# Another order for the first batch's preparation and the whole last batch, five weights' low parts on VectorE, and a wait on its own weights for each product

## The chip, the cores and the metric

The kernel runs on one core of a Trainium2 chip. The metric is the device time of one execution in microseconds (us). Five engines work in parallel, each through its own queue of instructions in order: TensorE (PE: matmuls and transposes; PEld is its weight load), VectorE (DVE), ScalarE (ACT), GpSimd (POOL) and SyncE (SP, which here issues the DMAs). They wait for one another by semaphores.

## The reference

x has 8 batches of 1024 tokens of 512 values. All tensors are float32.

```python
# attention-like part, on xn = layernorm(x)
s    = sigmoid(silu(xn @ s_w1.T + s_b1) @ s_w2.T + s_b2)        # 512 -> 256 -> 128
u    = (xn @ B_w.T + B_b) * s                                   # 128 states
h[t] = h[t-1] @ A.T + u[t]                                      # scan over the 1024 tokens
y    = h @ C_w.T + C_b + xn @ D_w.T + D_b
gate = sigmoid(xn @ g_w.T + g_b)
x1   = x + layernorm(y * gate)
# feed-forward part, on x2 = layernorm(x1)
z    = square(relu(x2 @ Ws1)) @ Ws2  + routed part
out  = x1 + layernorm(z)
```

The routed part is multiplied by the whole part of a softmax weight, so it is not zero only where one expert takes a weight of 1. A bound on the gap between router columns (`router_gap`, `route_flag`) says whether that can be, and with the given weights the branch that computes it is not entered.

## The kernel before

**Tiles.** A batch is 8 tiles of 128 tokens (index j, 0 to 7), in two halves of 4 tiles (index m). Each product of float32 values is made of three passes at the single-pass type: high part times high part, high times low, low times high (`mm3`, L428 to L430). So every weight needs a high part (ScalarE, `high_part`, L797) and a low part (raw minus high, `low_part`, L182), and every activation that goes into a product too.

**Work of one batch.** By the names in the code:
- `ln1_stats`, `ln1_norm` (VectorE, L1083 to L1099), with `ln1_rs` (GpSimd, L1533, a power) between them: the first layer norm, for the four tiles of a half at once in `ln1_rs`.
- `FT(j)` (TensorE, four transposes, L488), `ft_hi(j)` (ScalarE, L843), `ft_low(j)` (VectorE, L1161): the transposed tile in two parts.
- `H(m,f)` (12 matmuls over a half), `sig(m,f)` (ScalarE, L861), `h1(m,f)` (VectorE, L1177 and L1183), `h1_low(m,f)` (GpSimd, L1578), `B(m)` (12 matmuls), `SG(m)` (6 matmuls, L576 to L579), `s_gate(m)` (ScalarE, L869), `u_of(m)` (VectorE, L1192).
- The scan: 12 steps, each of a few small matmuls (`scan_step`) and one addition on VectorE (`scan_add`), strictly one after the other. Steps 5 to 11 give u[0] to u[6], and `hs(j)` (ScalarE), `hs_low(j)` (VectorE, L1137) split them for `Y`.
- `G(j)` (12 matmuls) and `gate(j)` (ScalarE, L812); `Y(j)` (15 matmuls: 12 of D, then 3 of C, which need `hs_low(j)`); `attn(j)` (VectorE, L1144, product and statistics), `v_rs(j)` (GpSimd), `attn_norm(j)` (VectorE, L1152), `x1(j)` (GpSimd, L1569, the residual), `x1_stats(j)` (VectorE), `x1_rs(j)` (GpSimd), `x1_norm(j)` (ScalarE, L835), `T(j)` (TensorE, four transposes), `t_hi(j)` (ScalarE, L830), `t_low(j)` (VectorE).
- `W1f(m,f)` (12 matmuls), `hidden(m,f)` (ScalarE, relu L852 and square L855), `h2(m,f)` (VectorE, L1207 and L1211), `W2(j)` (6 matmuls), `z_stats(j)` (VectorE), `z_rs(j)` (GpSimd), `zn(j)` (ScalarE, L874), `outs(j)` (GpSimd, L1573), store.

**Stages.** Before the first batch stands its preparation (layer norm, transposes, H, B, SG), together with 24 powers of A (`power(i)`, L438 on TensorE, `copy_power(i)`, L801 on ScalarE; each power needs the copy of the one before) and the parts of the weights. Then come `first_tail` and `body` for batch 0, `tail` and `body` for batches 1 to 6, and `last_tail`, `last_body` and a few last lines for batch 7. A `tail` holds the scan, G(0) to G(3) and the second half of the feed-forward part of the batch before; a `body` holds Y, G(4) to G(7), T, the first half of the feed-forward part and the preparation of the next batch. `last_tail` and `last_body` have no next batch to prepare. In each of these functions the order is written out by hand, for each engine.

**Buffers that set waits.** G, Y and z share three PSUM banks in a fixed ring (`TM_RING`, L209), T and FT two, H, B, SG and W1f two. `hs_hi` and `hs_lo` have two places. Raw weights lie in buffers that batches use later: s1, b, c, f1 and f2 in `work`, g and d in `xres`, s2 in `u`; so `gate(j)` of batch 0 waits for low parts that read `work[:, j]`, and the loads of `xres` (one_pass, L362) for those of g and d.

**Weights.** `less_first_of(name)` (VectorE, L1109) takes the first row off s1, b, g and d, and writes a bias into row 0 for g and d. The low parts of b and s2 are made on VectorE, those of s1, g, d, c, f1 and f2 on GpSimd. TensorE waits for the parts of s1, b, s2 before H, B, SG, for those of g before `first_tail`, and for all others, up to f2, before `body` of batch 0. VectorE too waits for the low part of f2 there.

**Order of the preparation before**, where pN is power(N), cN its copy, and hi and lo are parts of a weight:

```
PE   p0-5 FT0 p6 FT1 p7 FT2 p8 FT3 p9 p10 H00 p11 H01 p12 FT4 p13 B0 p14 FT5 p15 SG0 p16 FT6 p17 FT7 p18 p19
     H10 p20 H11 p21 B1 p22 SG1 p23 first_tail
ACT  c0-4 hi(s1) c5 ft_hi0 c6 ft_hi1 c7 ft_hi2 c8 ft_hi3 c9 c10 hi(b) hi(s2) hi(g) sig00 c11 sig01 c12 ft_hi4
     c13 c14 ft_hi5 c15 [wait less_first d] s_gate0 c16 ft_hi6 c17 ft_hi7 hi(d) c18 c19 sig10 c20 hi(c) hi(f1)
     sig11 c21 hi(f2) c22 s_gate1 c23 first_tail
DVE  stats0-3 norm0-3 less_first(s1) ft_low0 ft_low1 stats4 ft_low2 ft_low3 stats5 stats6 less_first(b) stats7
     lo(b) lo(s2) less_first(g) h1_00 norm4 h1_01 norm5-7 ft_low4 less_first(d) ft_low5 u_of0 ft_low6 ft_low7
     h1_10 h1_11 u_of1 first_tail
POOL rs0 lo(s1) rs1 h1_low00 h1_low01 lo(g) h1_low10 h1_low11 lo(d) lo(c) lo(f1) lo(f2)
```

## Time and profile before

| | |
|---|---|
| median of 3 runs | 909.72 us (908.83 to 910.61) |
| profiled execution | 909.91 us, span from first to last instruction 908.1 us |
| mean granted TensorE clock | 0.98 |
| busy in the span | PE 855.5, PEld 707.2, DVE 604.4, ACT 301.2, POOL 384.1 us |
| DMA | 73.23 MB, mean 81 GB/s |

The execution's own time is 1.8 us more than its span. Matmuls are pipelined, so a busy PE is not PE at its peak. The mean clock hides stages: a stretch of the trace runs at either 1.2 or 2.4 GHz, which the rows below show as a share of full speed (0.50 or 1.00, or a mixture where it changed inside).

### The profile page before, as it was taken

The page shows a single profiled execution, that of the slowest core. Times are in us where ns is not written, and L with a number is a line of the kernel's source. Part 1 is how long each engine was busy: PE and PEld are TensorE (multiplying, and loading weights), DVE is VectorE, ACT ScalarE, POOL GpSimd, SP SyncE. Part 2 cuts the span into 40 slices and gives each one's busy share as a digit, 9 for nine tenths or more (in the row PEclk, how much of TensorE's full clock was granted, in tenths as well). Part 3 has the DMA queues.
Part 4 walks back from the last instruction along what each step waited for, and adds up shares of the span by engine and source line. Part 5 has one row for each costly group of instructions (what it writes and reads, how often), then busy time and mean ns, then how long its engine had stood idle before and what let it go on. Part 6 is the DMA issues. An engine that isn't in the chain of part 4 may idle for free. (4 is left out here: it accounts for less than half of the span.)

```text
span 908.1 us, 12877 instructions
## 1 busy us (share of the span) xinstructions
PE 855.5 (94%) x4120; PEld 707.2 (78%) x4120; DVE 604.4 (67%) x1376; ACT 301.2 (33%) x530; POOL 384.1 (42%) x505
## 2 busy tenths in 40 slices
PE   5688999999999999999999999999999999999974
PEld 3566888888888888888888888888888888887763
DVE  4825677577766677577775777577785777744663
ACT  3241243323342233323343233332433233423332
POOL 1433344353461643444451633625443534605444
PEclk9879999999999999999999999999999999999987
DMA  9212022221132232302322220402222110122112
GB/s 296 75 49 92 1 93 93 93 70 52 65 117 71 93 92 80 107 24 70 93 93 94 93 90 19 150 22 93 93 93 94 61 75 4 70 70 93 48 46 93
DMA packets 17309, 73.23 MB, mean 81 GB/s; under 512 B 2643, under 2 KB 5075, under 8 KB 11094
## 3 DMA queue, kind: packets, MB, share of 16 engines
q1 hardware_dynamic: 17238, 72.38, 23.0%
q8 instruction: 33, 0.54, 0.3%
q14 instruction: 38, 0.31, 0.1%
HBM read 38.82 MB, written 33.55 MB: 80 GB/s over the span
## 5 line engine op out<-in xcount | busy, mean ns | idle before, releaser
L1533 POOL TENSOR_TENSOR rsz<-rsz,negh 128x1 f32<-128x1 f32 x64 | 39.9, 623 | 157.7 <-DVE rsz L1234 157.7
L428 PE MATMUL TM<-gw_hi,xT_hi 128*128 128x512 f32 x256 | 104.7, 409 | 0.7 <-ACT apt L801 0.7
L1569 POOL TENSOR_TENSOR xres<-work,xres 128x512 f32<-128x512 f32 x64 | 82.5, 1289 | 50.4 <-DVE work L1152 49.6
L428 PE MATMUL TM<-dw_hi,xT_hi 128*128 128x512 f32 x256 | 103.5, 404 | 0.0
L430 PE MATMUL TM<-dw_hi,xT_lo 128*128 128x512 f32 x256 | 100.6, 393 | 0.0
L430 PE MATMUL TM<-gw_hi,xT_lo 128*128 128x512 f32 x256 | 100.5, 393 | 0.0
L429 PE MATMUL TM<-dw_lo,xT_hi 128*128 128x512 f32 x256 | 100.1, 391 | 0.0
L429 PE MATMUL TM<-gw_lo,xT_hi 128*128 128x512 f32 x256 | 99.9, 390 | 0.0
L1533 POOL TENSOR_TENSOR rsv<-rsv,negh 128x1 f32<-128x1 f32 x64 | 35.9, 560 | 141.1 <-DVE rsv L1148 141.1
L1573 POOL TENSOR_TENSOR work<-work,xres 128x512 f32<-128x512 f32 x62 | 80.3, 1306 | 15.7 <-ACT work L874 15.7
L812 ACT ACTIVATE work<-TM 128x512 f32<-128x512 f32 x64 | 38.0, 594 | 121.3 <-PE TM L430 100.8
L874 ACT ACTIVATE work<-TM,nmz,rsz 128x512 f32<-128x512 f32 x62 | 48.3, 779 | 75.8 <-POOL nmz L1543 75.7
L1144 DVE TENSOR_TENSOR work<-TM,work 128x512 f32<-128x512 f32 x64 | 44.1, 689 | 39.9 <-PE TM L430 34.8
L830 ACT ACTIVATE x2T_hi<-TR 128x512 fp32r<-128x512 f32 x64 | 37.9, 594 | 77.6 <-PE TR L488 77.3
L1533 POOL TENSOR_TENSOR rsx<-rsx,negh 128x1 f32<-128x1 f32 x64 | 40.2, 628 | 54.0 <-DVE rsx L1158 54.0
L428 PE MATMUL TM<-f2w_hi,h_hi 128*128 128x512 f32 x124 | 51.8, 418 | 8.8 <-DVE h_lo L1211 6.9
L835 ACT ACTIVATE work<-xres,nmx,rsx 128x512 f32<-128x512 f32 x64 | 52.0, 812 | 24.2 <-POOL nmx L1543 24.2
L1578 POOL TENSOR_TENSOR h_lo<-hf,h_hi 128x512 fp32r<-128x512 f32 x32 | 41.7, 1303 | 38.5 <-DVE h_hi L1183 38.5
L430 PEld LDWEIGHTS TM<-dw_hi,xT_lo 128*128 128x128 f32 x256 | 48.3, 189 | 10.5
L430 PEld LDWEIGHTS TM<-gw_hi,xT_lo 128*128 128x128 f32 x256 | 48.0, 188 | 10.8
L428 PEld LDWEIGHTS TM<-gw_hi,xT_hi 128*128 128x128 f32 x256 | 48.2, 188 | 9.4 <-ACT apt L801 0.9
L429 PEld LDWEIGHTS TM<-dw_lo,xT_hi 128*128 128x128 f32 x256 | 48.5, 189 | 9.0
(145 smaller groups left out, 2104.4 us busy)
## 6 DMA issues: line engine op xcount, KB each, us to landing
...
```

Source lines behind the costliest of these rows:

```text
L428: eng.matmul(ps, lhs[0], rhs[0], start=first, stop=False)
L429: eng.matmul(ps, lhs[0], rhs[1], start=False, stop=False)
L430: return eng.matmul(ps, lhs[1], rhs[0], start=False, stop=last)
L812: eng.activation(work[:, j, :], tm_bank(f"g{j}")[:, :], ACT.Sigmoid).then_inc(S["gate_ok"], 1)
L830: eng.activation(x2T_hi[:, j % MS, :, :], tr_bank(f"t{j}")[:, :].rearrange("p (k n) -> p k n", n=P), ACT.Copy).then_inc(S["t_hi"], 1)
L835: eng.activation(work[:, j, :], xres[:, j, :], ACT.Identity, bias=nmx[:, j:j + 1], scale=rsx[:, j:j + 1])\
L874: eng.activation(work[:, j, :], z_bank(rep, j)[:, :], ACT.Identity, bias=nmz[:, j:j + 1], scale=rsz[:, j:j + 1]).then_inc(S["zn_ok"], 1)
L1144: eng.tensor_tensor(work[:, j, :], tm_bank(f"y{j}")[:, :], work[:, j, :], ALU.mult)\
L1533: return eng.tensor_tensor(dst, src, negh[:, 0:n], ALU.pow)
L1569: eng.tensor_tensor(xres[:, j, :], work[:, j, :], xres[:, j, :], ALU.add).then_inc(S["x1_ok"], 1)
L1573: eng.tensor_tensor(work[:, j, :], work[:, j, :], xres[:, j, :], ALU.add).then_inc(S["out_ok"], 1)
L1578: eng.tensor_tensor(h1_lo[:, f, :], hf_row(name), h1_hi[:, f, :].bitcast(F32), ALU.subtract).then_inc(S["h1lo_ok"], 1)
```

## The change

It does these things:
- The low parts of s1, g and d go from GpSimd to VectorE, so five are made there (s1, b, s2, g, d) and three on GpSimd (c, f1, f2).
- TensorE waits for the parts of each weight at the first product that reads them (`weights(name)`), and no longer for g before `first_tail` and for f2 before `body`. VectorE's wait for f2 goes. The wait for the copies of all powers stands at scan step 0. ScalarE's wait for less_first(d) before s_gate0 goes (it waits for that of g); VectorE adds the C and D biases by one operation of its own, `add_biases`, and d's row 0 is then a copy.
- The preparation, `first_tail`, `last_tail`, `last_body` and what follows them have another order on all four engines. `router_gap` moves on VectorE from before `last_tail` into it, and on TensorE from before the last four W2 to before the last one. `route_flag` stands before z_stats(7).
- The last z4 and z5 use other PSUM banks (TM[0] and TM[1] in place of TM[2] and TM[0]).

`tail` and `body`, which run batches 0 to 6, keep their order.

```
preparation after
PE   p0-5 FT0 p6 FT1 p7 FT2 p8 p9 FT3 p10-15 H00 FT4 p16 H01 B0 FT5 FT6 SG0 p17 FT7 p18 p19
     H10 p20 H11 p21 B1 p22 SG1 p23 first_tail
ACT  c0-5 hi(s1) ft_hi0 c6 c7 ft_hi1 c8-10 ft_hi2 c11-13 ft_hi3 c14 hi(b) c15 ft_hi4 hi(s2) sig00 hi(g) sig01
     c16 ft_hi5 ft_hi6 s_gate0 c17 ft_hi7 c18-20 sig10 c21 sig11 hi(d) hi(c) c22 hi(f1) c23 hi(f2) s_gate1
DVE  stats0-3 less_first(s1) norm0 norm1 lo(s1) norm2 ft_low0 norm3 stats4 stats5 ft_low1 stats6 ft_low2 ft_low3
     stats7 add_biases less_first(b) norm4 less_first(g) lo(b) h1_00 norm5 h1_01 norm6 lo(s2) ft_low4 ft_low5
     norm7 ft_low6 u_of0 ft_low7 lo(g) less_first(d) h1_10 h1_11 lo(d) u_of1 first_tail
POOL rs0 rs1 h1_low00 h1_low01 h1_low10 h1_low11 lo(c) lo(f1) lo(f2)
last_tail | last_body | what follows (norm is attn_norm)
PE   G0{s0} s1 W10{s2} W11{s3 s4} s5 G1{s6} s7 G2{s8} W2_4 s9 W2_5 s10 G3 W2_6 W2_7 s11 |
     Y0 G4 Y1 G5 Y2 G6 Y3 T0 G7 Y4 T1 Y5 T2 T3 Y6 W00 Y7 W01 T4 T5 W2_0 W2_1 T6 T7 W2_2 W2_3 |
     W10 W11 W2_4 W2_5 W2_6 router_gap W2_7
ACT  (body) hs2 hs3 gate4 x1_norm0 gate5 t_hi0 hs4 hs5 gate6 x1_norm1 x1_norm2 hs6 gate7 t_hi1 x1_norm3 hs7 t_hi2
     t_hi3 x1_norm4 hidden00 x1_norm5 t_hi4 hidden01 t_hi5 x1_norm6 x1_norm7 t_hi6 zn0 t_hi7 zn1 zn2 |
     hidden10 hidden11 zn3 zn4-7
DVE  (body) attn0 hs_low2 norm0 x1_stats0 attn1 hs_low3 attn2 norm1 norm2 x1_stats1 attn3 t_low0 norm3 x1_stats2
     hs_low4 x1_stats3 attn4 hs_low5 hs_low6 t_low1 norm4 attn5 t_low2 t_low3 norm5 hs_low7 x1_stats4 x1_stats5
     attn6 h2_00 norm6 attn7 x1_stats6 norm7 t_low4 h2_01 x1_stats7 t_low5 z_stats0 z_stats1 t_low6 t_low7
     z_stats2 z_stats3 | h2_10 h2_11 z_stats4-6 route_flag z_stats7 last residuals (j = 6, 7)
POOL (body) in pairs: v_rs0 x1_0 x1_rs0 v_rs1 x1_1 v_rs2 x1_2 x1_rs1 v_rs3 x1_3 x1_rs2 x1_rs3 v_rs4 x1_4 v_rs5 x1_5
     x1_rs4 x1_rs5 v_rs6 x1_6 v_rs7 x1_7 x1_rs6 x1_rs7 z_rs0 outs0 z_rs1 z_rs2 outs1 outs2 z_rs3 |
     outs3 z_rs4 z_rs5 outs4 outs5 z_rs6 z_rs7
```

The diff, cut to its core (of the orders only some stand here; the lists above hold the rest). The low parts, the banks and TensorE's waits and `first_tail`:

```diff
-        LO_DVE = {n: i + 1 for i, n in enumerate(["b", "s2"])}
-        LO_POOL = {n: i + 1 for i, n in enumerate(["constants", "s1", "g", "d", "c", "f1", "f2"])}
+        LO_DVE = {n: i + 1 for i, n in enumerate(["s1", "b", "s2", "g", "d"])}
+        LO_POOL = {n: i + 1 for i, n in enumerate(["constants", "c", "f1", "f2"])}
-        LAST_BANKS = dict(zip(range(MS, L), (TM[2], TM[0], *TR)))
+        LAST_BANKS = dict(zip(range(MS, L), (TM[0], TM[1], *TR)))
...
+            def weights(name):
+                eng.wait_ge(hi_ok, HI[name])
+                eng.wait_ge(*lo_of(name))
             def scan_step(b, rep, i):
+                if i == 0 and rep == 0:
+                    eng.wait_ge(pw_cp, len(POWERS))
...
             def G(b, rep, j, steps={}):
+                if rep == 0 and j == 0:
+                    weights("g")
             def Y(b, rep, j):
+                if rep == 0 and j == 0:
+                    weights("d")
+                    weights("c")
...
             def first_tail(b, rep):
-                G(*a, 0, {2: 0, 3: 1})
-                G(*a, 1, {0: 2, 1: 3, 2: 4, 3: 5})
-                G(*a, 2, {0: 6, 1: 7, 2: 8, 3: 9})
-                G(*a, 3, {0: 10, 1: 11})
+                G(*a, 0, {1: 0})
+                scan_step(*a, 1)
+                G(*a, 1, {0: 2, 1: 3, 2: 4})
+                scan_step(*a, 5)
+                G(*a, 2, {1: 6, 2: 7})
+                scan_step(*a, 8)
+                scan_step(*a, 9)
+                G(*a, 3, {0: 10})
+                scan_step(*a, 11)
...
-            eng.wait_ge(pw_cp, len(POWERS))
-            eng.wait_ge(hi_ok, HI["g"])
-            eng.wait_ge(lo_pool, LO_POOL["g"])
             first_tail(0, 0)
-            eng.wait_ge(hi_ok, HI["f2"])
-            eng.wait_ge(lo_pool, LO_POOL["f2"])
             body(0, 0)
```

VectorE's `first_tail` (up to step 8), `last_tail` (from step 6) and the end of `last_body`:

```diff
             def first_tail(b, rep):
                 scan_add(*a, 0)
                 ln1_stats(b + 1, 0)
                 scan_add(*a, 1)
+                ln1_stats(b + 1, 1)
                 scan_add(*a, 2)
-                ln1_stats(b + 1, 1)
+                ln1_stats(b + 1, 2)
                 scan_add(*a, 3)
                 scan_add(*a, 4)
+                ln1_stats(b + 1, 3)
                 scan_add(*a, 5)
                 scan_add(*a, 6)
-                ln1_stats(b + 1, 2)
+                ln1_norm(b + 1, 0)
                 scan_add(*a, 7)
-                ln1_stats(b + 1, 3)
                 scan_add(*a, 8)
...
             def last_tail(b, rep):
...
                 scan_add(*a, 6)
+                hs_low(*a, 0)
+                h2(*a, 1, 1)
                 scan_add(*a, 7)
+                router_gap()
                 scan_add(*a, 8)
-                hs_low(*a, 0)
                 scan_add(*a, 9)
                 z_stats(*a, 4)
+                z_stats(*a, 5)
                 scan_add(*a, 10)
-                hs_low(*a, 1)
-                z_stats(*a, 5)
-                scan_add(*a, 11)
                 z_stats(*a, 6)
                 z_stats(*a, 7)
+                hs_low(*a, 1)
+                scan_add(*a, 11)
             def last_body(b, rep):
...
                 attn(*a, 6)
+                h2(*a, 0, 0)
                 attn_norm(*a, 6)
-                h2(*a, 0, 0)
+                attn(*a, 7)
                 x1_stats(*a, 6)
-                attn(*a, 7)
                 attn_norm(*a, 7)
+                t_low(*a, 4)
                 h2(*a, 0, 1)
-                t_low(*a, 4)
                 x1_stats(*a, 7)
```

ScalarE, after `last_body`:

```diff
             hidden(NB, NB, 1, 0)
+            hidden(NB, NB, 1, 1)
             zn(NB - 1, NB - 1, 3)
-            hidden(NB, NB, 1, 1)
```

## Rows read from the trace of the kernel before

**Rows 1.** Busy us and (x) instructions by engine, PE's clock: first and last stretch.

```profile
110.00:210.00 100.00, 99.86 (x490) 82.91 (x489) 70.66 (x165) 33.39 (x59) 44.45 (x61) 1.00 0.24 85
...
710.00:790.00 80.00, 79.66 (x385) 66.05 (x383) 60.63 (x137) 28.34 (x50) 41.35 (x58) 1.00 0.14 53
```

**Rows 2.** Who waited for whom, PE: us in total, times, longest.

```profile
PE SC L438 <- ACT apt L801: 12.1, 7, 4.5
```

**Rows 3.** In order of time, PE, preparation: start, duration, what, [idle before].

```profile
7.95 0.79 PE L438 MATMUL SC<-apt,u 128*128 128x128 f32 x2 [0.37 <-ACT u L801]
9.11 0.79 PE L438 MATMUL SC<-apt,u 128*128 128x128 f32 x2 [0.37 <-ACT apt L801]
...
22.09 0.47 PE L428 MATMUL FM<-xT_hi,s1w_hi 128*128 128x512 f32 x1 [0.16 <-DVE xT_lo L1161]
...
51.47 0.77 PE L428 MATMUL FM<-xT_hi,s1w_hi 128*128 128x512 f32 x1
...
52.47 0.63 PE L430 MATMUL FM<-xT_hi,s1w_lo 128*128 128x512 f32 x1
52.90 0.63 PE L428 MATMUL FM<-xT_hi,s1w_hi 128*128 128x512 f32 x1
...
66.92 1.72 PE L448 MATMUL SC<-u,apt 128*128 128x128 f32 x14
...
86.42 1.08 PE L488 MATMUL TR<-ident,xin 128*128 128x128 f32 x4 [3.78 <-DVE xin L1099]
```

**Rows 4.** In order of time, ACT: copy_power(4), high_part(s1), s_gate(0).

```profile
12.26 0.28 ACT L801 ACTIVATE apt<-SC 128x128 f32<-128x128 f32 x1 [0.89 <-PE SC L438]
15.10 1.06 ACT L797 ACTIVATE s1w_hi<-work 128x1024 fp32r<-128x1024 f32 x1 [2.56 <-DVE work L1109]
...
45.82 0.69 ACT L869 ACTIVATE sg<-FM,b_col 128x512 f32<-128x512 f32 x1 [4.70 <-DVE xres L1116]
```

**Rows 5.** Groups, DVE, 0 to 66 us: shapes, count, busy, mean ns.

```profile
L1099 DVE TENSOR_SCALAR xin<-xin,mv,rs 128x511 f32<-128x511 f32 x8 | 9.1, 1192 | 1.2 <-issue 1.2
L1083 DVE BATCH_NORM_STATS2 st<-xin 128x6 f32<-128x512 f32 x8 | 5.5, 690 | 5.7 <-DMA xin<-in_x 5.1
L1109 DVE TENSOR_TENSOR xres<-xres,w_first 128x2048 f32<-128x2048 f32 x2 | 4.6, 2280 | 0.0
L1161 DVE TENSOR_TENSOR xT_lo<-TM,xT_hi 128x512 fp32r<-128x512 f32 x6 | 4.1, 686 | 4.2 <-ACT xT_hi L843 4.1
L1177 DVE SCALAR_TENSOR_TENSOR hf<-FM,b_col,hf 128x512 f32<-128x512 f32 x4 | 3.0, 750 | 11.6 <-ACT hf L861 11.6
```

**Rows 6.** In order of time, DVE norms, then POOL h1_low and lo(g).

```profile
35.48 6.68 DVE L1099 TENSOR_SCALAR xin<-xin,mv,rs 128x511 f32<-128x511 f32 x3
...
35.64 1.51 POOL L1578 TENSOR_TENSOR h_lo<-hf,h_hi 128x512 fp32r<-128x512 f32 x1 [0.36 <-DVE h_hi L1183]
37.11 4.76 POOL L182 TENSOR_TENSOR gw_lo<-xres,gw_hi 128x2048 fp32r<-128x2048 f32 x1
```

**Rows 7.** In order of time, PE, the last batch.

```profile
817.99 0.50 PE L428 MATMUL TM<-f2w_hi,h_hi 128*128 128x512 f32 x1 [1.24 <-ACT work L874]
...
854.47 0.63 PE L488 MATMUL TR<-ident,work 128*128 128x128 f32 x4 [1.98 <-ACT work L835]
...
867.29 1.03 PE L488 MATMUL TR<-ident,work 128*128 128x128 f32 x8
872.98 0.79 PE L428 MATMUL TM<-f2w_hi,h_hi 128*128 128x512 f32 x1 [4.66 <-DVE h_lo L1211]
...
882.65 0.39 PE L428 MATMUL FM<-x2T_hi,f1w_hi 128*128 128x512 f32 x1
...
888.12 1.00 PE L527 MATMUL SC<-w_first 128*128 128x64 f32 x8
891.38 0.78 PE L428 MATMUL TM<-f2w_hi,h_hi 128*128 128x512 f32 x1 [2.26 <-DVE h_lo L1211]
```

**Rows 8.** In order of time, DVE: the last residual.

```profile
904.14 0.69 DVE L1487 TENSOR_TENSOR work<-work,xres 128x512 f32<-128x512 f32 x1 [1.72 <-ACT work L874]
```

More of the change, by code:

```diff
@@ L511, in W1f @@
                     eng.wait_ge(S["t_lo"], body_at("t_lo", i, m * MS + MS - 1))
+                if rep == 0 and f == 0:
+                    weights("f1")
                 wait_free(eng, FM_RING, name, b, rep, FM_FREED)
@@ L536, in W2 @@
                     eng.wait_ge(S["h2lo_ok"], body_at("h2lo_ok", i, KF * m + KF - 1))
+                if rep == 0 and j == 0:
+                    weights("f2")
                 if rep < NB or j < MS + 2:
@@ L549, in H @@
                 name = f"h{m}{f}"
+                if rep < 0 and (m, f) == (0, 0):
+                    weights("s1")
                 if f == 0:
@@ L562, in B @@
                 js = slice(m * MS, (m + 1) * MS)
+                if rep < 0 and m == 0:
+                    weights("b")
                 wait_free(eng, FM_RING, f"b{m}", b, rep, FM_FREED)
@@ L569, in SG @@
             def SG(b, rep, m):
+                if rep < 0 and m == 0:
+                    weights("s2")
                 wait_free(eng, FM_RING, f"s{m}", b, rep, FM_FREED)
@@ L753, in _ @@
             last_body(NB - 1, NB - 1)
-            for f in range(KF):
-                W1f(NB, NB, 1, f)
+            W1f(NB, NB, 1, 0)
+            W1f(NB, NB, 1, 1)
+            W2(NB, NB, 4)
+            W2(NB, NB, 5)
+            W2(NB, NB, 6)
             router_gap()
-            for j in range(MS, L):
-                W2(NB, NB, j)
+            W2(NB, NB, 7)
             def routed_ffn(w1, w2):
@@ L859, in sig @@
                 eng.wait_ge(S["h_done"], prep_at("h_done", b + 1, KF * m + f))
+                if rep < 0 and (m, f) == (0, 0):
+                    eng.wait_ge(w_ld["small"], 3 * 16)
+                elif rep < 0 and (m, f) == (0, 1):
+                    eng.wait_ge(less_first, LESS_FIRST["b"])
                 wait_free(eng, HF_RING, name, b, rep, HF_FREED)
@@ L865, in s_gate @@
                 eng.wait_ge(S["s_done"], prep_at("s_done", b + 1, m))
+                if rep < 0 and m == 0:
+                    eng.wait_ge(less_first, LESS_FIRST["g"])
                 if m or rep >= 0:
@@ L1050, in _ @@
             hidden(NB, NB, 1, 0)
+            hidden(NB, NB, 1, 1)
             zn(NB - 1, NB - 1, 3)
-            hidden(NB, NB, 1, 1)
-            for j in range(MS, L):
-                zn(NB, NB, j)
+            zn(NB, NB, 4)
+            zn(NB, NB, 5)
+            zn(NB, NB, 6)
+            zn(NB, NB, 7)
             def routed_ffn():
@@ L1228, in route_flag, with last_outs @@
                    .then_inc(flag_ok, 1)
+            def last_outs(i):
+                j = L - 2 + i
+                eng.wait_ge(S["zn_ok"], body_at("zn_ok", NB - 1, j))
+                eng.tensor_tensor(work[:, j, :], work[:, j, :], xres[:, j, :], ALU.add).then_inc(last_out, 1)
             def z_stats(b, rep, j):
@@ L1476, in _ @@
                 body(b, 1)
-            router_gap()
             last_tail(NB - 1, NB - 1)
@@ L1481, in _ @@
             h2(NB, NB, 1, 1)
-            for j in range(MS, L):
-                z_stats(NB, NB, j)
-            for j in (L - 2, L - 1):
-                eng.wait_ge(S["zn_ok"], body_at("zn_ok", NB - 1, j))
-                eng.tensor_tensor(work[:, j, :], work[:, j, :], xres[:, j, :], ALU.add).then_inc(last_out, 1)
+            z_stats(NB, NB, 4)
+            z_stats(NB, NB, 5)
+            z_stats(NB, NB, 6)
             route_flag()
+            z_stats(NB, NB, 7)
+            last_outs(0)
+            last_outs(1)
             def routed_norm(dst, src):
```

317 lines of the change are left out of this document (167 added, 150 removed).

## Prediction, made before the changed kernel ran

> **What bounds the kernel now.** I read the busy time by stretch first. From 110 to 790 us, six middle batches, PE is busy for 99.86 of the first 100 us and 79.66 of the last 80, at a granted clock of 1.00, seven stretches alike [rows 1]. No order on another engine can shorten that part, and the change leaves it alone. So what can be won lies in the first 90 us and after 790. There I read PE's waits: 12.1 us for ScalarE's copies of powers, 7 times, 4.5 at most [rows 2], and then the instructions in order of time. In the preparation H(0,0) starts at 22.09, H(1,0) at 51.47, scan step 0 at 66.92, and FT(0) of the next batch, at 86.42, had waited 3.78 us for VectorE [rows 3]. H(1,0) is so late because of ScalarE's queue: s_gate(0) started at 45.82 after a wait of 4.70 for less_first(d) on VectorE [rows 4], and less_first(d) stood behind three norms that took 6.68 us together [rows 6]. In the last batch PE waits 1.24, 1.98, 4.66 and 2.26 us [rows 7]. Each stall of over 2 us costs twice: behind one, matmuls started 0.43 us apart (52.47 to 52.90) [rows 3], where 24 of them at full clock take 5.47 us (882.65 to 888.12), 0.23 each [rows 7].
>
> **The preparation up to H(0,0): a loss.** Before, powers 11 to 15 lay between products; now they stand ahead of H(0,0), and nothing covers them. One power and its copy are a round trip of 1.16 us (7.95 to 9.11) [rows 3]. Copy 4 starts at 12.26 [rows 4], copy 5 at 13.4; then hi(s1), 1.06 [rows 4], and one transposed high part of about 0.6 (estimate: a little under the 0.69 of s_gate) put copy 6 at 15.1. Nine more round trips, 10.4 us, bring power 15 to 25.5. ft_hi3 now stands behind copy 13, so ft_low3 ends at about 25.6, and H(0,0) starts at 26.2: 4.1 us later than before. lo(s1) is not late for it: half the columns of the VectorE pass that takes 2.28 us [rows 5], 1.2 us, from 14.7. The bounds of a round trip: its two durations alone, 0.79 and 0.28, give 1.07 (0.8 us less); if every one also waits for a high part of 0.6, 5.4 us more. I take 1.16, the row of the same pair of instructions.
>
> **From H(0,0) to H(1,0): the gain.** 24 matmuls, 5.5 us, with eight of them at the slow clock (8 x 0.2 = 1.6, since PE has had little to do before) and FT(4) with power 16 (0.8) end H(0,1) at 34.1. Then sig (0.7), h1 (0.75 and a cast of 0.4) [rows 5] and h1_low(0,1) with 1.51 [rows 6] run while PE does B(0), FT(5), FT(6). SG(0) starts at 39.0, since lo(s2) stands on VectorE behind norm6 and meets that h1_low. SG(0) 1.4, s_gate 0.7, u_of 0.75, ft_hi7 0.6, ft_low7 0.69 [rows 4, 5]: H(1,0) at 43.2, against 51.47, so 8.3 us earlier. What goes is the wait of s_gate(0) for less_first(d), and GpSimd's lo(g) of 4.76 us with the norms that stood still in it [rows 6]. lo(g) and lo(d) on VectorE have no row before; the nearest are less_first(g) and (d), the same columns and engine, 2.28 us each [rows 5], and GpSimd's 4.76 [rows 6] is the upper bound. I take 2.28.
>
> At this place a rule of the Trainium skill can be weighed. The row: three norms took 6.68 us while h1_low and lo(g) ran on GpSimd, and the other five of the eight, 9.1 - 6.68, took 0.48 each [rows 5, 6]. The Trainium skill (SBUF — State Buffer, section "SBUF: two separate sides") says that VectorE's two-port operations, and those with two SBUF inputs, share a port pair with GpSimd that one of them holds for its whole instruction. By that rule, the low parts now on VectorE stop GpSimd in turn, and lo(s2) waits for an h1_low as I put it; without the rule SG(0) and the sum would be 1.4 us earlier.
>
> **From H(1,0) to scan step 0.** 42 matmuls at 0.23 are 9.6 us, powers and starts add 1.2: power 23 ends at 54.0. Now ScalarE decides: s_gate(1) stands behind copy 23 and hi(f2). 0.3 + 1.06 + 0.7 + 0.75 [rows 4, 5] put u and step 0 at 56.8, against 66.92. Gain so far 10.1. On VectorE lo(g) runs at 43.1 to 45.4, less_first(d) with its row copy to 48.2, lo(d) ends at about 55.0; each is done before its product (G(0) at 54, Y(0) at 73), so they cost nothing while PE stays this late. If it were 9 us earlier, lo(g) would be the next to wait for. The new waits for single weights are met in the same way: c, f1, f2 on GpSimd (a quarter and twice a half of 4.76) end by 61.
>
> **first_tail and the next batch's FT(0).** Same 48 matmuls, same 12 steps; before they took 66.92 to 82.64 (86.42 less 3.78) [rows 3]. Steps 8 and 9 now stand together with nothing between: 0.3 us more. In return norm(0) of batch 1 stands behind scan_add 6 instead of 11 and behind statistics that fit between the steps (0.69 each and a small one) [rows 5], so FT(0) doesn't wait: 3.8 us, and the slow clock behind that wait, about seven matmuls and the transposes, 1.4 us. Start in all: 10.1 - 0.3 + 3.8 + 1.4 = **15.0 us**. The loads of xres can start earlier and nobody waits for them.
>
> **The last batch.** In last_tail W2(7) waited 1.24 us for zn(5) [rows 7]: z_stats(5) now stands ahead of scan_add 10 and hs_low(1): **1.2 us**. router_gap there takes about 2 us of VectorE between steps 7 and 8, while PE has three quarters of G(2): nothing. In last_body T(0) and T(1) come later, and x1_norm(3) stands ahead of hs(7), with GpSimd's work in pairs; by the same durations x1_norm(3) ends at about 851, before T(3) at 852.4, so 1.98 us go. Then h2(0,1) stands before x1_stats(7), and W2(0) waits about 2.7 us instead of 4.66: gain 4.0. Between W2(0) and W1f(1,0) another 0.64 of a wait for zn(0), by my placing of it, and three slow matmuls go: 1.2, so 5.2. hidden(1,1) no longer stands behind zn(3), and the router's product (1.00) [rows 7] leaves the gap between 888.12 and 891.38: 1.0 earlier, of which 0.5 comes back before W2(7). On GpSimd outs(5) stands before z_rs(6), 1.3 us that the others mostly hide: 0.3. The last residual, at 904.14 [rows 8], moves by 5.2 + 1.0 - 0.5 + 0.5 (a slow stretch a little shorter) - 0.3 = about **6 us**. The 0.64 and these halves are estimates from the same rows; a stall that isn't shortened takes them away, one that vanishes gives up to 2.7 more.
>
> **Sum.** 15.0 + 1.2 + 6.2 = 22.4 us. Against the profiled execution's 909.91 us that is 887.5. It stands 0.2 above the median of the runs shown (909.72), so I forecast 887.3.
>
> **Rivals.**
> - *The start gives half.* The round trips before H(0,0) take more than 1.16, or u(1) comes later behind hi(d), hi(c), hi(f1), hi(f2) and lo(d). For it: both chains are bare now, with 12.1 us of PE waits on copies already [rows 2]. Step 0 at 62 rather than 56.8, and a norm or two waiting for GpSimd: 5 to 9 us less gain, 893 to 897.
> - *The end gives nothing.* The last batch is a chain over five engines; if v_rs(2), now behind x1(1) on GpSimd, makes each hs_low late, PE waits at Y(4) to Y(7) for what it saved at T(3) and W2(0). 887.3 + 6 = 893.
> - *It doesn't do what it says.* PE bound in the middle could hold only if batch 1 needs something that comes at the old time, such as a load. The loads of x for batch 1 hang on FT(3) and FT(7) of batch 0, which come earlier. 909.7.
> - *Slower.* One mechanism in last_body: hs(4) stands on ScalarE behind t_hi(0), and that behind T(0), which PE now reaches only after Y(3); hs_low(4) on VectorE stands behind attn(3), norm3 and x1_stats(2), each behind a GpSimd step. If each of the five Y from Y(3) on waits for its hs_low, the change loses from 4.7 us apiece on (5 x 4.7 = 23.5, over the 22.4), which is the longest stall of the last batch before (4.66) [rows 7]: 911 and more. Against it: by my placing hs_low(4) is ready 0.7 us before Y(4) needs it.
>
> **How the numbers follow.** Forecast 0.61 (its own range 881 to 893: -1 to +3 at the round trips, 0 to 1.8 for the slow clock at each of three places, up to 2.7 at W2(0)); start gives half 0.20; end gives nothing 0.12; no effect 0.03; slower 0.04. The range reaches from 880 to 898 and leaves out some of the second rival with the last two. Faster 0.93, within 0.2% (about what a measurement of this kernel can tell) 0.03, slower 0.04.
>
> **What would show it.** In the profile after: H(0,0) near 26 and at the slow clock first; H(1,0) near 43; step 0 near 57; no wait for xin at FT(0); the middle still at 99% with 1.00; no wait of 1.98 at T(3); a wait under 3 us before W2(0); the last residual about 22 us earlier than 904. A step 0 later than 62, or waits for hs_low in the last Y, would make the forecast wrong.

## The result and the profile after

The changed kernel took **878.57 us** (median of 4 runs, 878.09 to 881.48) against 910.16 for the kernel before in the same session (4 runs), a ratio of 0.9662 with a 95% interval of 0.9638 to 0.9686. It is faster, as forecast, and by more than forecast: 31.6 us where 22.4 were summed, and below the range of 880 to 898. The profiled execution took 878.09 us, its span 876.3.

The page's line of busy time, and then who waited for whom on PE (us in total, times, longest):

```profile
PE 846.2 (97%) x4120; PEld 699.9 (80%) x4120; DVE 600.0 (68%) x1380; ACT 299.5 (34%) x530; POOL 374.5 (43%) x502
```

```profile
PE TM L433 <- DVE h_lo L1257: 4.4, 2, 2.3
...
PE SC L443 <- ACT apt L828: 2.4, 7, 0.4
...
PE SC L459 <- DVE u L1238: 1.4, 1, 1.4
PE TM L433 <- DVE hs_lo L1181: 1.1, 6, 0.2
```

The waits for copies of powers into `apt`, 12.1 us with one of 4.5 before [rows 2], are 2.4 now, seven of at most 0.4 (with the copies into `u` and `carry`: 15.1 before, 4.6 now). The waits for norms went from 4.6 to 0.3, the one of 2.0 at T(3) for x1_norm(3) is gone, and the two for h2's low part went from 6.9 to 4.4 us. The middle is nearly what it was: from 100 to 770 us PE is busy for 666.34 of 670 us (665.39 before), at a granted clock of 1.00; its one wait per batch for hs_low is 0.18 us in place of 0.34.

In order of time, PE in the preparation:

```profile
7.75 0.79 PE L443 MATMUL SC<-apt,u 128*128 128x128 f32 x2 [0.37 <-ACT u L828]
8.91 0.79 PE L443 MATMUL SC<-apt,u 128*128 128x128 f32 x2 [0.37 <-ACT apt L828]
...
19.36 0.49 PE L443 MATMUL SC<-apt,u 128*128 128x128 f32 x2 [0.37 <-ACT carry L828]
20.22 0.49 PE L443 MATMUL SC<-apt,u 128*128 128x128 f32 x2 [0.37 <-ACT apt L828]
...
23.23 0.56 PE L433 MATMUL FM<-xT_hi,s1w_hi 128*128 128x512 f32 x1
23.59 0.63 PE L434 MATMUL FM<-xT_lo,s1w_hi 128*128 128x512 f32 x1
24.02 0.63 PE L435 MATMUL FM<-xT_hi,s1w_lo 128*128 128x512 f32 x1
...
35.36 0.47 PE L602 MATMUL FM<-h_hi,s2w_hi 128*128 128x512 f32 x1 [0.52 <-issue]
...
39.15 0.50 PE L433 MATMUL FM<-xT_hi,s1w_hi 128*128 128x512 f32 x1
...
52.76 1.80 PE L459 MATMUL SC<-u,apt 128*128 128x128 f32 x14 [1.37 <-DVE u L1238]
68.89 0.60 PE L504 MATMUL TR<-ident,xin 128*128 128x128 f32 x4
69.29 0.47 PE L433 MATMUL TM<-dw_hi,xT_hi 128*128 128x512 f32 x1
```

And in the last batch, with VectorE's last residual behind it:

```profile
843.96 1.03 PE L504 MATMUL TR<-ident,work 128*128 128x128 f32 x8
847.29 0.50 PE L433 MATMUL TM<-f2w_hi,h_hi 128*128 128x512 f32 x1 [2.30 <-DVE h_lo L1257]
847.63 0.40 PE L434 MATMUL TM<-f2w_lo,h_hi 128*128 128x512 f32 x1
...
853.83 0.39 PE L433 MATMUL FM<-x2T_hi,f1w_hi 128*128 128x512 f32 x1
...
861.57 0.50 PE L433 MATMUL TM<-f2w_hi,h_hi 128*128 128x512 f32 x1 [2.15 <-DVE h_lo L1257]
861.91 0.39 PE L434 MATMUL TM<-f2w_lo,h_hi 128*128 128x512 f32 x1
```

```profile
872.33 0.69 DVE L1279 TENSOR_TENSOR work<-work,xres 128x512 f32<-128x512 f32 x1 [0.29 <-ACT work L908]
```

Set against rows 3, 7 and 8, in us of the span (the gain in the last column is before less after):

| | before | forecast | after | gain |
|---|---|---|---|---|
| H(0,0) | 22.09 | 26.2 | 23.23 | -1.1 |
| H(1,0) | 51.47 | 43.2 | 39.15 | 12.3 |
| scan step 0 | 66.92 | 56.8 | 52.76 | 14.2 |
| FT(0) of batch 1 | 86.42 | | 68.89 | 17.5 |
| scan step 0 of the last batch | 792.51 | | 772.85 | 19.7 |
| transposes ahead of W2(0) | 867.29 | | 843.96 | 23.3 |
| W2(0) | 872.98 | | 847.29 | 25.7 |
| W1f(1,0) | 882.65 | | 853.83 | 28.8 |
| W2(4) | 891.38 | | 861.57 | 29.8 |
| last residual | 904.14 | | 872.33 | 31.8 |

So the start gave 19.7 us where 15.0 were summed, and the end 12.1 where 7.4 were. Two things in the rows stand out. The power round trip is 1.16 us early (7.75 to 8.91), as in the row that I used, but 0.86 later (19.36 to 20.22): the two matmuls take 0.49 in place of 0.79, the wait for the copy 0.37 both times. And behind the last two waits the matmuls follow at 0.23 us (granted clock 1.00), where before seven and then six of them stood 0.43 apart (granted clock 0.50). Such a run of matmuls 0.43 us apart is called a slow stretch below.

### The profile page after: what moved, and what is told of

The parts are those of the page before. It is cut to its first block and busy times, and to the rows that moved or that the text cites. A ratio compares the mean times of both kernels' runs of the same rounds, so it can differ in the third digit from the quotient of the medians.

```text
span 876.3 us, 12884 instructions
## 1 busy us (share of the span) xinstructions
PE 846.2 (97%) x4120; PEld 699.9 (80%) x4120; DVE 600.0 (68%) x1380; ACT 299.5 (34%) x530; POOL 374.5 (43%) x502
## 5 line engine op out<-in xcount | busy, mean ns | idle before, releaser
L1628 POOL TENSOR_TENSOR work<-work,xres 128x512 f32<-128x512 f32 x62 | 79.5, 1293 | 17.5 <-ACT work L908 17.5
L1188 DVE TENSOR_TENSOR work<-TM,work 128x512 f32<-128x512 f32 x64 | 44.0, 688 | 30.6 <-PE TM L435 29.8
L434 PEld LDWEIGHTS TM<-gw_lo,xT_hi 128*128 128x128 f32 x256 | 48.3, 189 | 8.7
L433 PEld LDWEIGHTS TM<-dw_hi,xT_hi 128*128 128x128 f32 x256 | 48.1, 188 | 8.8
```

Source lines behind the costliest of these rows:

```text
L433: eng.matmul(ps, lhs[0], rhs[0], start=first, stop=False)
L434: eng.matmul(ps, lhs[0], rhs[1], start=False, stop=False)
L1188: eng.tensor_tensor(work[:, j, :], tm_bank(f"y{j}")[:, :], work[:, j, :], ALU.mult)\
L1628: eng.tensor_tensor(work[:, j, :], work[:, j, :], xres[:, j, :], ALU.add).then_inc(S["out_ok"], 1)
```

## Experiments

All are timed against the kernel before on the same chip (909.74 to 910.26 there), and "the changed kernel" is the 878.57 above, four executions that were not repeated beside the experiments. Ratios are to the kernel before, with 95% intervals; the changed kernel's is 0.9638 to 0.9686, so a difference from it of under about 2 us is not told apart from nothing by the medians alone. A comparison inside two profiles says more, but each is one execution.

### One end of the change at a time

**e1_last_only** is the kernel before with the new `last_tail`, `last_body`, what follows them, and the new banks. **e2_start_only** is the changed kernel with the old ones.

In e1 every engine has the new end behind the old preparation and `first_tail`; in e2 every engine has the old end behind the new preparation, `first_tail`, low parts and waits. The banks, in e1:

```diff
-        LAST_BANKS = dict(zip(range(MS, L), (TM[2], TM[0], *TR)))
+        LAST_BANKS = dict(zip(range(MS, L), (TM[0], TM[1], *TR)))
```

> The kernel before with only the new order of the last batch (last_tail, last_body and what follows, on all four engines, and the two banks). Theory: the changed kernel gained 19.7 us up to scan step 0 of the last batch (792.51 to 772.85) and 12.1 after it (31.8 at the last residual), and the two are independent, so this gives 910.2 - 12.1 = 898. Rival: my forecast's 7.4 is what the order gives, and the other 4.7 (slow-clock stretches behind the two last stalls that did not come) was luck of one execution or hangs on the start: 902.8, with matmuls 0.43 us apart behind a stall of over 2 us in the last batch.

> The changed kernel with the old order of the last batch, so only the preparation, first_tail, the low parts on VectorE and the waits for single weights are new. Theory of independent parts: 910.2 - 19.7 = 890.5. Rival (the start gives what I forecast, 15.0, and the middle batches gave the rest in one execution only): 895.

Measured: e1 899.49 us, ratio 0.9879 (0.9862 to 0.9895), a gain of 10.8. e2 889.15, ratio 0.9771 (0.9755 to 0.9787), 21.1. Together 31.9, against 31.6 for the whole change: the two ends add up, and each gave more than its part of the sum (7.4 and 15.0). "The end gives nothing" and "the start gives half" are both out. How the gain divides holds only within some 1.4 us, the size of a slow stretch: e1's profile has one behind W2(0), where the changed kernel's has none, and e2's has none behind W2(4), where the profile of before has one.

### Parts of the start

**e3_old_first_tail**: the changed kernel with the old order of `first_tail` on PE, ScalarE and VectorE.

VectorE, cut:

```diff
                 scan_add(*a, 6)
-                ln1_norm(b + 1, 0)
+                ln1_stats(b + 1, 2)
                 scan_add(*a, 7)
...
                 scan_add(*a, 11)
                 ln1_stats(b + 1, 5)
                 ln1_stats(b + 1, 6)
                 ln1_stats(b + 1, 7)
+                ln1_norm(b + 1, 0)
+                ln1_norm(b + 1, 1)
+                ln1_norm(b + 1, 2)
```

> The changed kernel with the old first_tail on all engines. Theory: norm(0) of batch 1 again stands behind scan_add 11 on VectorE, so FT(0) waits 3.8 us and the clock falls behind that wait (1.4): 878.6 + 5.2 - 0.3 = 883.5. Rival: first_tail was late before because the scan started late and weights were late; then the old order costs nothing here: 878.6.

887.56 us, ratio 0.974 (0.9719 to 0.9761): 9.0 us slower than the changed kernel, where the theory had 4.9. PE's rows have the wait back, with its slow clock:

```profile
73.63 1.08 PE L504 MATMUL TR<-ident,xin 128*128 128x128 f32 x4 [3.78 <-DVE xin L1134]
74.36 0.78 PE L433 MATMUL TM<-dw_hi,xT_hi 128*128 128x512 f32 x1
74.94 0.63 PE L434 MATMUL TM<-dw_lo,xT_hi 128*128 128x512 f32 x1
...
79.20 0.58 PE L435 MATMUL TM<-dw_hi,xT_lo 128*128 128x512 f32 x1
79.62 0.39 PE L433 MATMUL TM<-cw_hi,hs_hi 128*128 128x512 f32 x1
```

From 74.94 to 79.62 eleven matmuls stand 0.43 apart (granted clock 0.50), 0.2 us too many each: 2.2 us. That number is this execution's. Behind the same wait the kernel before had five:

```profile
88.58 0.63 PE L428 MATMUL TM<-dw_hi,xT_hi 128*128 128x512 f32 x1
89.01 0.53 PE L429 MATMUL TM<-dw_lo,xT_hi 128*128 128x512 f32 x1
89.38 0.39 PE L430 MATMUL TM<-dw_hi,xT_lo 128*128 128x512 f32 x1
```

From FT(0) to the first C product of Y(0) it is 5.99 us in e3, 4.56 in the kernel before and 3.25 in the changed kernel. From scan step 0 to that of the last batch e3 takes 726.14 us in place of 720.09, so the order of `first_tail` costs 6.0 us here. The profiled execution (888.47) is 10.4 us over the changed kernel's (878.09); the rest of that is slow stretches behind both last waits, 3.0 (next part but one), and 1.3 up to H(0,0), of which 1.1 is the load that power(0) waits for (7.73 in place of 6.59), not the edit.

**e4_early_waits** brings the early waits back: g ahead of `first_tail`, d and f2 ahead of `body` on PE, f2 on VectorE.

```diff
+            weights("g")
             first_tail(0, 0)
+            weights("d")
+            weights("f2")
             body(0, 0)
```

> The changed kernel with TensorE's old waits back: for g before first_tail, for d and f2 before body, and VectorE's for f2 before body. Theory: all of them are over by then (lo(f2) ends at 56.8, FT(0) starts at 68.9, lo(g) ends at 41.3, G(0) starts at 49.75), so 878.6. Rival (waiting for each product's own weights is a part of the gain): over 880.5.

878.82 us, ratio 0.9667 (0.9647 to 0.9686). No cost: each low part is done before either wait. The part "each product waits for its own weights" brings nothing in this order.

**e6_lows_on_pool** gives GpSimd the low parts of s1, g and d again.

```diff
-        LO_DVE = ... ["s1", "b", "s2", "g", "d"]
-        LO_POOL = ... ["constants", "c", "f1", "f2"]
+        LO_DVE = ... ["b", "s2"]
+        LO_POOL = ... ["constants", "s1", "g", "d", "c", "f1", "f2"]
```

> The changed kernel (878.6) with the low parts of s1, g and d back on GpSimd and all else as changed. Theory (the engine of these three matters: lo(g) took 4.76 us on GpSimd before, and VectorE's norms stood still for 6.68 in it): SG(0) or H(1,0) some 3 us later, 881 to 884. Rival (the order of the powers and products did it all, and the engine of the low parts nothing): 878.6.

886.35 us, ratio 0.9751 (0.9736 to 0.9767): 7.8 us slower, more than the theory's 2.4 to 5.4. GpSimd, and VectorE beside it:

```profile
34.51 4.72 POOL L186 TENSOR_TENSOR gw_lo<-xres,gw_hi 128x2048 fp32r<-128x2048 f32 x1
```

```profile
35.95 3.57 DVE L1139 TENSOR_SCALAR xin<-xin,mv,rs 128x511 f32<-128x511 f32 x1
```

The norm takes 3.57 us in place of 0.54 and ends 0.3 behind lo(g) (39.23). FT(6) waits 2.88 for it, H(1,0) comes at 41.70 (2.5 later) with a slow stretch behind it, and step 0 at 56.82 (4.1 later). Scan step 0 of the last batch is at 779.13, 6.3 later, and the end has a slow stretch behind W2(0), 1.5. The 2.2 between the two steps are not the low parts: those are made by 63.4. They come from one wait for hs_low in each of the six middle batches, at 199.96 and then every 104.8 us, 0.5 us in place of 0.2, and that from VectorE's own queue, which stands idle longer at one place of a batch whose order is the same. e6, then the changed kernel:

```profile
196.68 0.18 DVE L1124 BATCH_NORM_AGGREGATE mvv<-st 128x2 f32<-128x6 f32 x1 [0.50 <-DVEq L1120]
```

```profile
192.25 0.18 DVE L1124 BATCH_NORM_AGGREGATE mvv<-st 128x2 f32<-128x6 f32 x1 [0.15 <-DVEq L1120]
```

It is 0.50 and 0.15 in each of the six. What makes it so, no run shows. So by these profiles the engine of the low parts is worth 4.1 us of the start's 19.7, all of it before step 0, and the rest of the change there some 15.6; the 7.8 of the medians also holds the middle batches and the slow stretch. The Trainium skill (SBUF — State Buffer, section "SBUF: two separate sides") has VectorE's two-port operations shut out for a whole GpSimd instruction; the trace agrees, and in the changed kernel in both directions. There lo(d) meets h1_low(1,1), which GpSimd ends at 48.88, and GpSimd's lo(c) then meets lo(d); in e10, where it doesn't, lo(c) takes 1.32:

```profile
48.12 2.92 DVE L186 TENSOR_TENSOR dw_lo<-xres,dw_hi 128x2048 fp32r<-128x2048 f32 x1 [0.60 <-ACT dw_hi L824]
```

```profile
48.84 3.33 POOL L186 TENSOR_TENSOR cw_lo<-work,cw_hi 128x512 fp32r<-128x512 f32 x1
```

### The clock at the start

**e5_fillers** puts one unused matmul (into a bank that is overwritten) behind each of powers 9 to 15, which keeps PE busy during the copies. For power 9:

```diff
             power(9)
+            filler()
```

> The changed kernel (878.6) with one more matmul of 128x128 behind each of powers 9 to 15, in PE's waits of 0.37 us for the copies; its result goes to a bank that is overwritten. Theory (H(0,0)'s first nine matmuls are slow only because PE had little to do before): H(0,0) at 23.2 as before but its first matmuls 0.23 apart instead of 0.43, 1.6 to 1.8 us won, most of it kept up to scan step 0 only if ScalarE's chain there also moves: 877.0 to 878. Rival (the extra matmuls lengthen the round trips of 0.855 by 0.1 to 0.3 each, 1 to 2 us over seven): H(0,0) at 24 to 25 and 878.6 or more.

Busy time, granted clock next to last but two, from 23 to 27 us, in e5 and then in the changed kernel:

```profile
23.00:27.00 4.00, 3.73 (x19) 2.67 (x17) 3.46 (x9) 0.88 (x3) 1.38 (x1) 1.00 1.08 381
```

```profile
23.00:27.00 4.00, 4.00 (x12) 3.05 (x12) 3.47 (x9) 0.80 (x2) 1.38 (x1) 0.57 0.90 325
```

The slow matmuls of H(0,0) are gone, as the theory said, yet the time is 879.9 us (877.72 to 881.23), ratio 0.9669 (0.9655 to 0.9683): nothing won. From H(0,0) to SG(0) it is 11.63 us in place of 12.13, so of my 1.6 us for eight slow matmuls 0.5 were to be had; the rest lay beside other engines' work: B(0) now waits 0.48 us for h1(0,0), which stands on VectorE behind less_first(g), 2.28 us from 26.91 on. H(0,0) itself is at 23.86, 0.63 later, and so SG(0) is at 35.49 (35.36 without the fillers). The fillers don't do that: from power 11 on a round trip takes 0.86 us as without them (the rival's 0.1 to 0.3 more didn't come), but power 9, which stands ahead of the first of them, starts at 18.14 in place of 17.65, since PE reached the upper level later here. And this profile has a slow stretch behind W2(0), 1.5 us, which has nothing to do with the edit.

**e9_sgate_first** puts s_gate(1) ahead of hi(f2); **e10_sgate_d_pool** also gives lo(d) to GpSimd.

```diff
-            high_part("f2")
             s_gate(-1, -1, 1)
+            high_part("f2")
```

> The changed kernel (878.6) with s_gate(1) ahead of the high part of f2 on ScalarE. Theory (step 0 waits 1.37 us for u(1), that for s_gate(1) at 51.15, that for the high part of f2, 1.05): s_gate(1) about 0.95 earlier, u(1) then bound by lo(d), which ends at 51.04 on VectorE, so step 0 0.8 earlier: 877.8. Rival (lo(c) and lo(d), 3.33 and 2.92 beside each other, hold u(1) back anyway): 878.6.

> As the last one, and the low part of d on GpSimd ahead of that of c. Theory (u(1) is then free at s_gate(1)'s end): step 0 at 51.4 to 51.8, 877.2 to 877.6. Rival (GpSimd, as with three low parts on it, where PE waited 3.2 us for hs_lo in place of 1.1, is the bound behind step 0: its low parts end some 3 us later): the gain is given back in the first body, 878.6 to 880.7.

e9 took 878.97 us (ratio 0.9672, 0.9656 to 0.9687), e10 878.83 (0.9662, 0.9649 to 0.9675), with the lowest execution at 877.22 and the profiled one. The wait at step 0 shrank from 1.37 to 0.47 and 0.43, and from H(0,0) to step 0 it is 28.5 and 28.4 us in place of 29.5, but the medians don't show that microsecond. e9's profile says what hid it there: H(0,0) at 24.49. Of e10's rival the profiles show 0.3 us: from step 0 to that of the last batch 720.42 in place of 720.09, and its waits for hs_low are 1.1 us as in the changed kernel (those of e6 were not the low parts' doing, as above). What hid e9's gain stands in the profile of e7 (below) too, whose edit is 840 us later:

```profile
19.91 0.49 PE L443 MATMUL SC<-apt,u 128*128 128x128 f32 x2 [0.37 <-ACT carry L828]
20.76 0.53 PE L443 MATMUL SC<-apt,u 128*128 128x128 f32 x2 [0.37 <-ACT apt L828]
21.66 0.79 PE L443 MATMUL SC<-carry,apt 128*128 128x128 f32 x2 [0.37 <-ACT apt L828]
22.82 0.79 PE L443 MATMUL SC<-apt,carry 128*128 128x128 f32 x2 [0.37 <-ACT u L828]
```

The clock fell at 21 rather than at 23 (granted clock from 21 to 24 us 0.51), and the round trips behind it cost 1.16 us instead of 0.86. The order is the same. In the ten profiles with this order and no fillers (changed kernel, e2 to e4, e7 to e12) H(0,0) is anywhere from 22.99 to 24.55, and two things differ from one execution to the next: where the clock changes, and when the load that power(0) waits for is there (6.53 to 7.06 us, and 7.73 in e3).

### The clock and the orders at the end

**e7_gap_back** has `router_gap` ahead of W2(4) again, on PE alone. **e8_zn3_back** has ScalarE's zn(3) ahead of hidden(1,1) again.

e7, PE, and then e8, ScalarE:

```diff
+            router_gap()
             W2(NB, NB, 4)
             W2(NB, NB, 5)
             W2(NB, NB, 6)
-            router_gap()
```

```diff
             hidden(NB, NB, 1, 0)
+            zn(NB - 1, NB - 1, 3)
             hidden(NB, NB, 1, 1)
-            zn(NB - 1, NB - 1, 3)
```

> The changed kernel (878.6) with the router's product back ahead of W2(4), on PE alone. Theory (my forecast, which credited 1.0 us to moving it, of which 0.5 came back): W2(4) starts later by 0.5 to 1.0, 879.1 to 879.6. Rival (the product of 1.0 us lies inside the wait of 2.15 for h_lo and costs nothing there; what won the microsecond is ScalarE's zn(3), now behind hidden(1,1)): W2(4) at its old place, W2(7) 0.45 earlier, 878.1 to 878.6.

> The changed kernel (878.6) with zn(3) back ahead of hidden(1,1) on ScalarE, nothing else. Theory (this order is what shortened PE's idle time before W2(4), 3.26 with the router's product in it to 2.15): the wait before W2(4) grows by 0.8 to 1.1, 879.4 to 879.7, and with it a slow stretch of 1.6 us is likelier. Rival (the product's place did it): 878.6.

e7: 879.75 us (877.89 to 882.03), ratio 0.9666 (0.9649 to 0.9683). W2(4) follows the last product of W1f(1,1) in the same time as in the changed kernel, since the product lies inside the wait, which is 1.31 us now:

```profile
862.52 1.00 PE L545 MATMUL SC<-w_first 128*128 128x64 f32 x8
864.82 0.50 PE L433 MATMUL TM<-f2w_hi,h_hi 128*128 128x512 f32 x1 [1.31 <-DVE h_lo L1257]
```

and from W2(4) to the last residual it is 10.73 us (10.76 in the changed kernel). So the product's place, to which I gave 1.0 less 0.5, is worth nothing either way. e8: 882.05 us (880.92 to 882.57), ratio 0.9696 (0.9682 to 0.9709), 3.5 slower in the medians and 2.8 in the profiles: the wait before W2(4) grows to 3.12, 1.0 more, and eight matmuls behind it are 0.43 apart, 1.6 us. From W1f(1,0) to W2(4) it is 8.72 us there, 8.73 in the kernel before and 7.74 in the changed kernel. zn(3) behind hidden(1,1) is what won the microsecond, and in this profile more with the clock.

**How often the slow stretch comes.** Orders and waits at the end are alike in many of these kernels, so their profiles are repeats:

| wait | profiles | with 5 to 8 matmuls at 0.43 us behind it |
|---|---|---|
| 2.30, before W2(0) | 10 | 5 (e1, e3, e5, e6, e7) |
| 2.14 or 2.15, before W2(4) | 8 | 2 (e3, e4) |
| 2.26 (before), 2.28 (e2), before W2(4) | 2 | 1 (before) |
| 3.12 (e8), 4.66 (before, e2) | 3 | 3 |

So behind a wait of 2.14 to 2.30 us it came in 8 of 20. In e4 it begins 1.3 us after the product started:

```profile
860.62 0.50 PE L433 MATMUL TM<-f2w_hi,h_hi 128*128 128x512 f32 x1 [2.15 <-DVE h_lo L1260]
860.95 0.39 PE L434 MATMUL TM<-f2w_lo,h_hi 128*128 128x512 f32 x1
...
861.88 0.48 PE L435 MATMUL TM<-f2w_hi,h_lo 128*128 128x512 f32 x1
862.16 0.63 PE L433 MATMUL TM<-f2w_hi,h_hi 128*128 128x512 f32 x1
```

The granted clock, next to last but two, says that this is the clock and not a wait:

```profile
860.60:862.10 1.50, 1.48 (x6) 1.24 (x7) 0.00 (x0) 0.00 (x0) 1.20 (x1) 0.98 0.00 0
862.20:865.50 3.30, 3.30 (x9) 2.60 (x8) 1.57 (x4) 0.62 (x1) 0.81 (x2) 0.51 0.39 159
```

**e11_busy_stalls** puts six unused matmuls into each of the two waits; **e12_sgate_busy** has s_gate(1) earlier as well.

```diff
                 T(*a, 5)
+                busy(6)
                 W2(*a, 0)
...
             W1f(NB, NB, 1, 1)
+            busy(6)
             W2(NB, NB, 4)
```

> The changed kernel (878.6) with six matmuls of 128x128 put into each of PE's two last waits, ahead of W2(0) and W2(4), into a bank nobody reads there. Theory (a slow stretch of up to 8 matmuls, 1.6 us, comes behind these waits in some executions and not in others, as the profiles of the kernels above show; PE kept busy has none): no stretch at 0.43 us apart behind either, and the executions between 877.5 and 880, the median 878.0 to 878.6 with less scatter than 878.1 to 881.5. Rival (the scatter of 3 us comes from elsewhere, such as the start): the same scatter as before, 878.6.

> s_gate(1) ahead of the high part of f2, and the matmuls in both waits. Theory (the two add): 877.2 to 877.8, the candidate to beat the changed kernel. Rival (neither is on the path): 878.6.

e11: 878.12 us, ratio 0.9658 (0.9645 to 0.9671), four of its five executions from 877.74 to 878.3 and one at 880.55. No slow stretch at the end of its profile. The interval lies within the changed kernel's, and the changed kernel's own profile had no slow stretch either, so a gain from the fillers isn't shown. e12: 877.32 (876.93 to 879.4), ratio 0.9653 (0.964 to 0.9666). It differs from e11 by s_gate(1) alone and was timed on the same chip: step 0 is at 51.85 in place of 52.79, the last residual at 871.26 in place of 872.27, and the medians are 0.8 apart, though the executions overlap.

**e13_before_busy** does it to the kernel before: 13 and 6 unused matmuls in its two last waits, all orders untouched.

```diff
+                busy(13)
                 W2(*a, 0)
...
             router_gap()
+            busy(6)
```

> The kernel before with matmuls of 128x128 in PE's two last waits (13 ahead of W2(0), where it waits 4.66 us, 6 ahead of W2(4)), orders and waits untouched. Theory (the slow clock behind these waits was on the path to the end, 7 matmuls at 0.2 us each in the profile of before): no matmuls 0.43 us apart behind them, 1.4 to 2.8 us won, 907 to 908.5. Rival (the chain over the other engines, not PE's pace, sets the end): 909.8.

909.29 us, ratio 0.9992 (0.9983 to 1.0001): 0.7 us, which isn't told apart from nothing, and half of the theory's least. PE's rows:

```profile
870.63 3.07 PE L442 MATMUL SC<-ident 128*128 128x128 f32 x26
...
873.85 0.50 PE L428 MATMUL TM<-f2w_hi,h_hi 128*128 128x512 f32 x1 [0.15 <-DVE h_lo L1217]
...
882.03 0.50 PE L428 MATMUL TM<-f2w_hi,h_hi 128*128 128x512 f32 x1 [2.50 <-ACT work L880]
...
892.88 0.50 PE L428 MATMUL TM<-f2w_hi,h_hi 128*128 128x512 f32 x1
```

The two waits tell different things. The stretch behind W2(0) is gone and nothing is won there: PE waits 2.50 us at W2(3) for zn(0), in place of 0.64, and the clock falls behind that, so that W1f(1,0) comes 10.14 us after W2(0) in place of 9.67. ScalarE's zn(0) starts 7.35 us after W2(0) here and 7.33 in the kernel before, at either clock; in the changed kernel it is 4.19. The kernel before and then the changed kernel:

```profile
880.31 0.78 ACT L874 ACTIVATE work<-TM,nmz,rsz 128x512 f32<-128x512 f32 x1 [2.62 <-POOL nmz L1543]
```

```profile
851.48 0.78 ACT L908 ACTIVATE work<-TM,nmz,rsz 128x512 f32<-128x512 f32 x1
```

So before the change the path there went over the other engines (x1_norm(7), which waited 3.4 us for GpSimd, t_hi(5), t_low(5), z_stats(0), z_rs(0), zn(0)), not over PE. Behind W2(4) it is otherwise: with the stretch gone, the last residual (904.08) comes 11.20 us after W2(4), in place of 12.76. That stretch was on the path, 1.56 us. Over the whole last batch, from step 0 to the last residual, the profile has 110.76 us in place of 111.63, 0.9 less.

**e14_sgate_busy_fill** is e12 with one unused matmul behind each of powers 10 to 15.

```diff
             power(10)
+            filler()
```

> s_gate(1) ahead of the high part of f2, matmuls in both last waits, and one behind each of powers 10 to 15. Theory (what scatter is left comes from the clock at the start, where a fall ahead of power 13 costs 0.3 us per round trip): the executions within 1.5 us of each other, the median 876.9 to 877.3. Rival (the scatter is in what PE waits for elsewhere): 876.9 to 879.4 as without them.

876.64 us, ratio 0.9637 (0.9624 to 0.9651): three executions from 876.51 to 876.64, two at 878.43 and 878.5. It is 1.9 us below the changed kernel in the medians; the two intervals still overlap a little (0.9638 to 0.9651). The scatter didn't go: in the profiled execution, at 878.5, PE's pace reached the upper level only at 22 us (17 in the changed kernel), with PE busy for all of 20 to 22, and H(0,0) came at 25.13. In this profile and in e5's no matmul of H(0,0) is slow, in the ten without fillers six or seven are at 0.43. So matmuls between the powers kept the clock up once it had risen, but it still rose late here.

## Why the prediction was outside its range

The direction, both mechanisms and most of the places were right; terms of the sum were wrong, nearly all to one side. The start was 4.7 us too small (19.7 for 15.0) and the end 4.7 (12.1 for 7.4). Two steps failed: the price of a power round trip ahead of H(0,0), and "each stall of over 2 us costs twice", which kept slow stretches in the sum behind both last waits, and the first of them as PE's path.

- **The preparation up to H(0,0): a size wrong, 3.0 us.** "I take 1.16, the row of the same pair of instructions." It is the same pair, but a row at 8 us, and by 17 us PE ran at the upper of its two levels: seven of the nine round trips took 0.86, and from copy 6 (15.1 forecast, 15.09 measured) to the end of power 15 (23.27) it is 8.2 us, not 10.4. That is 2.2 of the 3.0. The other 0.7 is a gap that the sum left between power 15 (25.5) and H(0,0) (26.2) without a row for it; there is none. The evidence on the pace was in the trace of before: power 10 took 0.49 there, at 21.44. My lower bound of 1.07 was "its two durations alone", at the slow durations, so it was no bound: 0.86 is under it.
- **From H(0,0) to step 0: right within 1.1 us** (30.6 summed, 29.5 measured). The slow matmuls came as forecast and H(0,1) took as long as summed, 7.9 us from H(0,0); the 1.1 too many stand behind it, 0.6 up to SG(0) and 0.4 from there to H(1,0). "lo(s2) ... meets that h1_low" was right: it takes 1.49 us at 33.77, where it took 0.42 alone before. But it ends at 35.26, 0.3 behind h1_low(0,1) (34.97), which SG(0) at 35.36 needs too: by these rows it costs about 0.3, not the 1.4 put on it. "u and step 0 at 56.8" because of s_gate(1) behind hi(f2) was the right link: the wait is there, 1.37 us, and goes with the order (e9).
- **Low parts of s1, g and d on VectorE: right**, at 2.28 us for g; d takes 2.92, of which 0.64 beside h1_low(1,1). Their engine is worth 4.1 us up to step 0 (e6).
- **FT(0) of batch 1: right**, 3.4 by the rows for 3.8 less 0.3. **The slow clock behind it: right**, 1.3 for 1.4 (4.56 us from FT(0) to the first C product before, 3.25 after); e3 drew a longer one. **The batches after it: 0.8 where I had nothing.** "The change leaves it alone" holds for their order, not quite for their time: the wait for hs_low fell from 0.34 to 0.18 per batch, and e6 shows the same wait at 0.5. The cause is open.
- **Weights waited for one by one: nothing, as put** (e4).
- **last_tail, 1.2: right** (1.5, up to T(2)). **T(3) and W2(0): right**, 4.5 for 4.0; the wait is 2.30 where I had 2.7.
- **W2(0) to W1f(1,0): a size wrong, 1.9 us** (1.2 summed, 3.1 measured, 9.67 to 6.54). I kept a slow stretch behind W2(0) and took PE's pace for the path. Before, the path went over x1_norm(7) and zn(0) (e13). In the changed kernel t_hi(5) stands ahead of x1_norm(6) and x1_norm(7) on ScalarE, z_stats(0) starts 1.7 us after W2(0) in place of 4.9, and zn(0) is there in time; that this order did it is read from the rows, no run has it alone. The profile of after has neither a wait nor a slow matmul there. In e5, where the stretch did come, W2(0) to W1f(1,0) took 8.06: in the new order it is on the path, 1.5 us.
- **W2(4) to the end: 2.0 where I had -0.3.** I kept its slow stretch too. It cost 1.6 of the 12.76 us before (e13 has 11.20 without it), 1.3 and 1.5 where it came in the new order (e4, e3), and here it didn't come. That part of the 31.6 is luck of the draw, and so are up to 1.5 us behind W2(0). "router_gap leaves the gap: 1.0" was the wrong cause of a right size; the microsecond is zn(3)'s (e7, e8).
- **A slip in the sum, 0.3 the other way:** the end's terms add up to 5.9 (5.2 + 1.0 - 0.5 + 0.5 - 0.3), and the sum carries 6.2.

None of the rivals came. The range was too narrow where the terms were: it allowed "-1 to +3 at the round trips" when they took 2.2 less, and it took the slow clock at the end as a quantity that goes with the length of the wait. It is rather a chance: the profile of after drew none at two places, and its execution is the lowest of the four. Two such stretches are worth 3 us, twice what the median lies below the range (878.57 under 880).

What stays open: how the 15.6 us of the start without the low parts' engine divide over the moved powers, s_gate(0) without less_first(d), and the rest of the order, since they were not run apart; what sets VectorE's idle time in the middle batches; and whether a shorter last chain over ScalarE and GpSimd is to be had in the last batch, which wasn't tried.
